# A second attention of its own: scores and maxima of two heads on the two row halves of TensorE, 1,024-column maxima, three score banks

## The chip, the cores and the metric

The kernel runs on one core of one Trainium2 chip. The metric is the device time of one execution in microseconds (us); lower is better. The core has TensorE for matmuls (PE in the rows, PEld for its weight loads), VectorE (DVE), ScalarE (ACT), GpSimd (POOL) and SyncE (SP). Each works through its own queue in order, and they wait for each other through semaphores. PSUM has eight banks of 512 f32 columns per partition.

## The reference, cut to what matters

A batch of 8 images of 32 x 32 positions with 192 channels passes through two attentions and a mixture of 16 experts. Both attentions have 12 heads of 16 channels and attend over the 1,024 positions of an image. The change is in the second one alone:

```
t = x.reshape(8, 1024, 192)
q, k, v = heads(ln(t) @ Wq + bq), heads(ln(t) @ Wk + bk), heads(ln(t) @ Wv + bv)
scores = einsum('bhqd,bhkd->bhqk', q, k) / sqrt(192)
t = t + (softmax(scores) @ v)
```

`L1_attn_ref` has `S = 1024` here, so each of the 96 (image, head) pairs has a 1024 x 1024 score matrix. The softmax needs the largest score of each query before it exponentiates.

## The kernel before

**Stages.** Projection and first attention (with position terms), projection and second attention, a router and the experts. `attention()` serves both attentions; `rel=False` is the second, and all that follows speaks of that one.

**Steps and blocks.** A step is one image and four heads (`GH = 4`), so there are `STEPS = 24` of them, two per trip of a loop (`ITERS = 12`; the first and the last trip are written out). A step has 16 blocks: a block is one tile of 128 keys (`kt`) against 512 queries (`qh`), for the four heads.

**Operands.** Queries and keys are kept as sums of two f16 parts, so a product has several terms, one for each pair of parts, stacked along the contraction: four terms of 16 rows here, 64 rows, and one more row (65) that subtracts the maximum, in the query operand `A`, against a constant row in `K`. A separate set of operands, `AM` and `KM`, feeds the maxima, with two heads on rows 0 to 63 and two on rows 64 to 127.

**Scores and exponentials.** In each block PE computes four heads' scores, 512 columns each, as two pairs (`scores_pair`, L371) into `psS`, four banks, two pairs deep: pair n waits until the exponential of pair n - 2 is done. ACT takes a pair in one instruction of 1,024 columns (L458) into `probs`. The product with the values (`pv`, L382) comes one block later: four heads in f32 on the four column groups of 32, eight matmul instructions in the trace, accumulating into the one bank `psO`.

**Maxima.** They are computed one step ahead, in the layout with queries on the partitions: 64 jobs per step, each one matmul of 512 keys (L353) into a ring of three banks, `psR`, and one DVE reduction of 512 columns (L503). Four jobs run in each block. When all 64 are done, DVE combines halves (L508), PE transposes the 32 columns once (`rows`, L357), DVE scales them (L513), and SP writes them by DMA into row 64 of `A` (L266). Each step also has two `back` jobs, one per query half: ACT copies `psO` out (L449), PE transposes it (four transposes, L361), DVE divides by the row sum (L520, L523), SP stores it.

**Order on PE in a block.** Both score pairs, two maxima jobs, `pv` of the block before, two more maxima jobs, then a `back` or `rows` job where there is one. The prologue, before step 0, has 77 jobs: all 64 of step 0, its `rows`, and 12 of step 1. The last step has no maxima left to compute.

**Loads.** POOL issues the DMAs for the next step one block at a time, each after a `pv`: eight of 128 KB for `A` and `K` (L185, L186), two for the values, and sixteen of 64 KB for `AM` and `KM` (L201, L202).

Of the kernel before, what the change touches and what calls it, by code (L numbers as in the profile page):

```python
# [6 lines left out]
F32 = mybir.dt.float32  # L7
F16 = mybir.dt.float16
I32 = mybir.dt.int32
ALU = mybir.AluOpType  # L10
ACT = mybir.ActivationFunctionType
AX = mybir.AxisListType

P = 128
# [4 lines left out]
GH = 4  # L19
# [23 lines left out]
def attention(nc, name, rel, scale, QK, RL, RLH, VN, OD, onehot_dram, head, early=None):  # L43
# [13 lines left out]
    with ExitStack() as ctx:  # L57
# [86 lines left out]
        def base_of(i):  # L144
            return BASE1 + (i - 1) * N_BODY
# [347 lines left out]
        @block.vector  # L493
        def _(dve):
            nc.vector.sem_inc(pvdone, 2)
            nc.vector.sem_inc(ring_free, 3)

            def job(jn, j, base, slot, buf, steps):
                dve.wait_ge(ring_full, base + jn + 1)
                if j[0] == "max":  # L500
                    r, half, p, qt, unit = max_of(j[1])
                    mx = MX[(buf + j[2]) % 2]
                    nc.vector.tensor_reduce(mx[:, unit, half:half + 1], psR[:, slot, :], AX.X, ALU.max)\  # L503
                        .then_inc(ring_free, 1)
                    if j[1] == HALVES - 1:

                        dve.wait_ge(ring_free, base + jn + 4)
                        nc.vector.tensor_tensor(MC[:, :], mx[:, :, 0], mx[:, :, 1], ALU.max).then_inc(maxed, 1)  # L508
                elif j[0] == "rows":

                    if steps is not None:
                        dve.wait_ge(mrow, steps * (16 * NROW) + 16 * NROW)
                    nc.vector.tensor_scalar(MT[:, :], psR[0:UNITS, slot, 0:P], -1.0 / MAXSCALE, None, ALU.mult)\  # L513
                        .then_inc(ring_free, 1)
                else:

                    qh, half = j[2], steps * QH + j[1] * QH + j[2]
                    o = psR[:, slot, :].rearrange("p (x v) -> p x v", v=VW)
                    dve.wait_ge(ring_free, base + jn + 3)
                    nc.vector.reciprocal(RC[:, :, :], o[:, :, HD:HD + 1]).then_inc(recips, 1)  # L520
                    dve.wait_ge(recips, half + 1)
                    dve.wait_ge(stored[qh], steps * 16 + (16 * j[1] + 16))
                    nc.vector.tensor_tensor(OS[:, qh, :, :], o[:, :, 0:HD], RC[:, :, :].to_broadcast([P, 4 * GH, HD]),  # L523
                                            ALU.mult).then_inc(ring_free, 1)

            for n, j in enumerate(FIRST):
                job(n, j, 0, first_slot(n), 0, None)

            def step(i, u, jobs, base, slot):
                for js in jobs[u]:  # L530
                    for jn, j in js:
                        job(jn, j, base, slot(jn), u, 2 * i + u)

            for u in range(2):
                step(0, u, JOBS_FIRST, BASE0, lambda n: first_slot(BASE0 + n))
            with dve.Fori(1, ITERS - 1) as i:
                for u in range(2):
                    step(i, u, JOBS, base_of(i), slot_of)
            for u in range(2):
                step(ITERS - 1, u, JOBS_LAST, base_of(ITERS - 1), slot_of)  # L540

def project(nc, name, first, IN, W, CONST, QK, VN, head, RL=None, RLH=None, ON=None, X2=None):
# [1088 lines left out]
class Head:  # L1632

    def __init__(self, nc, ctx, name, rel, QK, RL, RLH, onehot):
        def sb(n, shape, dt):
            return ctx.enter_context(nc.sbuf_tensor(f"{name}_{n}", shape, dt))

        def sem(n):
            return ctx.enter_context(nc.semaphore(f"{name}_{n}"))  # L1640

        self.rel, self.QK, self.RL, self.RLH, self.onehot = rel, QK, RL, RLH, onehot
        self.AM = [sb(f"qmax0_{h}", [P, 2, L], F16) for h in range(2)] if rel else [sb("qmax0", [P, 2, L], F16)] * 2
        self.KM = sb("kmax0", [P, 2, L], F16)
        self.MX = sb("halfmax0", [P, GH * KT, 2], F32)
        self.MC = sb("rowmax", [P, GH * KT], F32)
        self.MT = sb("rowmaxT", [GH * KT, P], F16)
        self.ident = sb("ident", [P, P], F32)
        self.loadedm = sem("loadedm0")
        self.const_km = sem("const_km0")  # L1650
        self.qkst, self.vst, self.xst = sem("qkst"), sem("vst"), sem("xst")
        self.last = sem("last")
        self.XST = ROUNDS * 384 - 192 + 16 if rel else ROUNDS * 64 + 16
        self.LAST = 96 + (192 if rel else 0)

    def wait_projected(self, engine):
# [2 lines left out]
        engine.wait_ge(self.xst, self.XST)  # L1659
        engine.wait_ge(self.last, self.LAST)  # L1660

    def load(self, pool):

        def pair(part, kind, r):
            return self.QK[0, part, kind].rearrange("(r p d) t -> r d p t", p=2, r=2)[r]
# [2 lines left out]
            k, t = rows.shape  # L1669
            return rows.rearrange("k (o t) -> k o t", o=1).to_broadcast([k, n, t])  # L1670

        KM, onehot = self.KM, self.onehot
        pool.wait_ge(self.qkst, 192 + 16)
        pool.wait_ge(self.vst, 96 + 16)
        if not self.rel:
            for n, (a, k) in enumerate(((0, 0), (0, 1), (1, 0), (1, 1))):
                for r in range(2):
                    of = slice(64 * r + HD * n, 64 * r + HD * n + HD)
                    pool.dma_start(self.AM[0][of, :, :], pair(a, 0, r)).then_inc(self.loadedm, 16)
                    pool.dma_start(KM[of, :, :], pair(k, 1, r)).then_inc(self.loadedm, 16)  # L1680
            return
        for r in range(2):
            at = 64 * r + HD
            pool.dma_start(KM[at:at + WI, :, :], every(onehot[HI:REL, :], 2)).then_inc(self.const_km, 16)
            for half in range(2):
                cols = slice(512 * half, 512 * half + 512)
                pool.dma_start(KM[at + WI:64 * r + 64, :, cols], every(onehot[16 * half:16 * half + 16, cols], 2))\
                    .then_inc(self.const_km, 16)
# [45 lines left out]
def hybrid_block(nc, a, out):  # L1734
# [21 lines left out]
    with ExitStack() as ctx:  # L1756
        head = Head(nc, ctx, "h2", False, QK2, None, None, a["onehot"])
        project(nc, "p2", False, a["x"], {"wqk": a["a_wqk"], "bqk": a["a_bqk"], "wv": a["a_wv"], "bv": a["a_bv"],
                                          "proj_w": a["proj_w"], "proj_b": a["proj_b"]}, const, QK2, VN2, head,
                ON=O1, X2=X2)  # L1760
        early = Early(nc, ctx, X2, ((a["w1"], a["b1"]), (a["w2"], a["b2"])))
        TR = ctx.enter_context(nc.sbuf_tensor("f_tileExpert", [1, P], I32))
        IXA = ctx.enter_context(nc.sbuf_tensor("f_slotsAll", [P, NTILE], I32))
        attention(nc, "a2", False, 1.0 / float(np.sqrt(C)), QK2, None, None, VN2, O2, a["onehot"], head, early)
        route(nc, "r", early, O2, a["wg"], a["bg"], X3, SLOTS, TR, IXA)
        experts(nc, "e", X3, early.W, early.wl, early.WDONE, TR, IXA, out)

# [51 lines left out]
```

## Time and profile before

| | |
|---|---|
| time, median of 3 runs | 3236.21 us (3226.59 to 3236.48) |
| the profiled execution: span, first to last instruction | 3278.2 us |
| mean granted TensorE clock | 0.906 of full speed |
| second attention: first maxima matmul to last transpose | 1750.0 to 2844.8 us |
| PE, DVE, ACT busy in 2000 to 2100 us | 99.6, 97.0, 73.0 us |

A row of the timeline gives the start, the length, the engine and line, output from input, and the number of like instructions that it merges; in square brackets, how long the engine had sat idle and what released it.
### The profile page before, as it was taken

How to read it: one execution, taken by the hardware profiler on the slowest of the kernel's cores; microseconds unless marked ns; L12 is line 12 of the kernel's file. 1: busy time of each engine (PE TensorE's matmuls, PEld its weight loads, DVE VectorE, ACT ScalarE, POOL GpSimd, SP SyncE). 2: the span in 40 equal slices, each digit the busy share in tenths (PEclk: the TensorE clock that was granted, in tenths of full speed). 3: DMA queues.
4: the chain of work that ended last, by engine and by line, in shares of the span. 5: the costliest groups of instructions: out<-in, count | busy, mean ns of one | idle time of the engine just before them, and what ended most of it. 6: DMA issues, size and time to landing. Idle time of an engine off the chain costs nothing. (4 is left out here: it accounts for less than half of the span.)

```text
span 3278.2 us, 63755 instructions
## 1 busy us (share of the span) xinstructions
PE 2922.2 (89%) x17818; PEld 1147.0 (35%) x17818; DVE 2439.8 (74%) x4430; ACT 1849.7 (56%) x2379; POOL 1061.6 (32%) x1714
## 2 busy tenths in 40 slices
PE   5886999999999999977897999999999999871887
PEld 4664122222222222215652222222222222361666
DVE  4544899999999999933547999999999999451221
ACT  2433376667776677663440677777777777610332
POOL 0012233333333333213232333232333332155665
PEclk9776799999999999998995999999999999965777
DMA  6776554555445554433654622222222222350211
GB/s 126 219 237 184 104 103 98 100 110 107 102 101 100 111 103 100 90 61 121 206 160 98 124 72 70 72 75 75 73 76 75 70 71 63 97 89 12 58 54 35
DMA packets 222364, 327.92 MB, mean 100 GB/s; under 512 B 63820, under 2 KB 150550, under 8 KB 217650
## 3 DMA queue, kind: packets, MB, share of 16 engines
q0 software_dynamic: 79488, 202.00, 27.3%
q1 hardware_dynamic: 142772, 124.60, 14.5%
q8 instruction: 56, 0.92, 0.1%
q14 instruction: 48, 0.39, 0.1%
HBM read 217.71 MB, written 109.19 MB: 100 GB/s over the span
## 5 line engine op out<-in xcount | busy, mean ns | idle before, releaser
L458 ACT ACTIVATE a_probs<-a_psS 128x1024 f32<-128x1024 f32 x1536 | 1488.5, 1021 | 738.5 <-PE a_psS L371 734.0
L503 DVE TENSOR_REDUCE h_halfmax<-a_psR 128x1 f32<-128x512 f32 x1536 | 979.7, 686 | 73.5 <-PE a_psR L353 64.3
L503 DVE TENSOR_REDUCE a_halfmax<-a_psR 128x1 f32<-128x512 f32 x1536 | 984.2, 686 | 63.6 <-PE a_psR L353 54.5
L371 PE MATMUL a_psS<-a_qrows,a_krows 121*128 121x512 f16 (+1 forms) x3072 | 804.2, 383 | 44.8 <-DMA a_qrows<-relh 40.2
L382 PE MATMUL a_psO<-a_probs,a_v 128*32 128x512 f32 x6144 | 824.0, 609 | 1.2 <-ACT a_probs L458 1.2
L353 PE MATMUL a_psR<-h_kmax,h_qmax 64*128 64x512 f16 x1536 | 357.9, 405 | 40.8 <-POOL h_ident L39 40.1
L371 PEld LDWEIGHTS a_psS<-a_qrows,a_krows 121*128 121x128 f16 (+1 forms) x3072 | 241.8, 98 | 417.7 <-issue 161.5
L353 PE MATMUL a_psR<-a_kmax,a_qmax 64*128 64x512 f16 x1536 | 325.6, 393 | 1.8 <-DVE a_halfmax L503 1.4
L353 PEld LDWEIGHTS a_psR<-h_kmax,h_qmax 64*128 64x128 f16 x1536 | 81.9, 93 | 539.1 <-DVE h_halfmax L503 471.6
L353 PEld LDWEIGHTS a_psR<-a_kmax,a_qmax 64*128 64x128 f16 x1536 | 78.9, 93 | 490.4 <-DVE a_halfmax L503 460.1
L185 POOL DMA_DIRECT2D a_qrows<-qk x240 | 124.1, 517 | 264.5 <-PE a_psO L382 262.0
L861 PE MATMUL p_psQ<-p_xnT,p_wqk 96*128 96x512 f32 x384 | 183.0, 640 | 16.0 <-DVE p_xnT L1015 13.9
L382 PEld LDWEIGHTS a_psO<-a_probs,a_v 128*32 128x32 f32 x6144 | 121.2, 108 | 183.3 <-issue 176.3
L201 POOL DMA_DIRECT2D h_qmax<-qk x110 | 56.3, 512 | 358.4 <-PE a_psO L382 305.2
L1628 DVE TENSOR_TENSOR e_y<-e_psY,e_x 128x192 f32<-128x192 f32 x80 | 28.6, 357 | 191.1 <-PE e_psY L1553 106.6
L201 POOL DMA_DIRECT2D a_qmax<-qk x120 | 61.4, 512 | 301.3 <-PE a_psO L382 300.5
L1049 DVE SCALAR_TENSOR_TENSOR p_half<-p_qk,p_sc,p_half 128x2048 f16<-128x2048 f32 (+1 forms) x36 | 71.5, 1997 | 103.1 <-ACT p_half L958 103.1
L951 ACT ACTIVATE p_qk<-p_psQ,p_bqk 128x512 f32<-128x512 f32 x96 | 65.9, 686 | 114.6 <-PE p_psQ L861 114.6
L1590 ACT COPY e_xmT<-e_psX 96x256 f32<-96x256 f32 x80 | 29.5, 369 | 175.0 <-PE e_psX L1547 130.5
L861 PEld LDWEIGHTS p_psQ<-p_xnT,p_wqk 96*128 96x128 f32 x384 | 77.5, 206 | 117.1 <-issue 107.3
L190 POOL DMA_DIRECT2D a_qrows<-rel x96 | 48.6, 506 | 205.6 <-PE a_psO L382 205.6
L197 POOL DMA_DIRECT2D a_v<-v x96 | 53.8, 560 | 185.4 <-PE a_psO L382 184.7
(185 smaller groups left out, 2755.2 us busy)
## 6 DMA issues: line engine op xcount, KB each, us to landing
a_qrows<-qk POOLq DMA_DIRECT2D x240, 128.0 KB, 4.2
qk<-p_half SPq DMA_DIRECT2D x96, 256.0 KB, 3.3
a_qrows<-rel POOLq DMA_DIRECT2D x96, 256.0 KB, 4.2
a_v<-v POOLq DMA_DIRECT2D x96, 256.0 KB, 3.1
a_krows<-qk POOLq DMA_DIRECT2D x168, 128.0 KB, 4.5
v<-p_v SPq DMA_DIRECT2D x36, 512.0 KB, 5.7
relh<-p_rel SPq DMA_DIRECT2D x48, 256.0 KB
attn<-a_out SPq DMA_DIRECT2D x96, 128.0 KB, 2.3
```

Of the source, the lines that this page charges most:

```text
L185: pool.dma_start(A[buf][c][at, :, :], qk(s, TERMS[n][0], 0)).then_inc(loaded[buf], 16)
L190: pool.dma_start(A[buf][c][w:w + WI, :, :], rel_w(s, half)).then_inc(loaded[buf], 16)
L197: pool.dma_start(V[buf][:, x, :, :], VN[s][:, x, :, :]).then_inc(loaded[buf], 16)
L201: pool.dma_start(AM[buf][0][of, :, :], qk_pair(s, TERMS[n][0], 0, r)).then_inc(loadedm[buf], 16)
L353: mm = nc.tensor.matmul(psR[:, slot, :], AM[b][half][at, p, P * qt:P * qt + P], KM[b][at, p, 512 * half:512 * half + 512], start=True, sto ...
L371: mm = nc.tensor.matmul(psS[:, (2 * n + j) % 4, :], K[buf][:, h, keys], A[buf][kt % NA][:, h, queries], start=True, stop=True)
L382: mm = nc.tensor.matmul(psO[32 * h:32 * h + 32, :], V[buf][:, kt, h, :], PT[:, blk % 2, h, :], start=(kt == 0), stop=(kt == KT - 1))
L458: nc.scalar.activation(PT[:, blk % 2, 2 * pair:2 * pair + 2, :], psS[:, b0:b0 + 2, :], ACT.Exp, scale=scale).then_inc(exped, 1)
L503: nc.vector.tensor_reduce(mx[:, unit, half:half + 1], psR[:, slot, :], AX.X, ALU.max)\
L861: mm = nc.tensor.matmul(psQ[:, n % 2, :], WQK[:, c, P * m:P * m + P], XN[:, c, 512 * q:512 * q + 512], start=(c == 0), stop=(c == 1))
L951: nc.scalar.activation(QF[:, m, 512 * q:512 * q + 512], psQ[:, n % 2, :], ACT.Identity, bias=BQK[:, m:m + 1], scale=1.0).then_inc(qf, 1)
L1049: half = nc.vector.scalar_tensor_tensor(HL[1][:, m, tokens], QF[:, m, tokens], SC[:, m:m + 1], HL[0][:, m, tokens], ALU.mult, ALU.subtract)
```

## The change

The second attention gets a function of its own, `attention_pairs`; the first keeps `attention()`.

- Three terms instead of four: 48 rows, 49 with the maximum's row. Heads 0, 1 lie on rows 0 to 48 and heads 2, 3 on rows 64 to 112, so that two heads' matmuls can run side by side. The same operands `A` and `K` serve scores and maxima; `AM` and `KM` are gone.
- Maxima: a job is two matmuls, one per row half, into 1,024 columns (two banks) of a ring of two, and one DVE reduction of 2 x 512 columns. There are 32 jobs per step, two per block, and the prologue has 22.
- Scores: two heads at a time, into a ring of three banks, and ACT takes one head of 512 columns per instruction. A pair of score matmuls waits until the first head of the pair before it has been exponentiated. The order in a block is: pair, maxima job, pair, maxima job (and `back`), `pv`.
- The maxima's row is made in two halves per step, after blocks 5 and 13: four small transposes into a score bank, an ACT copy, two DMAs.
- The twelve loads of `A` and `K` for the next step, 64 KB each, are issued together at the step's start; PE waits for them at block 5. The values are loaded after blocks 6 and 8.

```diff
+def attention_pairs(nc, name, scale, QK, VN, OD, onehot_dram, head, early):
+    TERMS = ((0, 0), (0, 1), (1, 0))
+    R = len(TERMS) * HD
+    HALF = PAIRS * 2 * KT // QH
+    PER_BLK = QH * HALF // BLK
+    NEXT = 5
+    AHEAD = NEXT + HALF // PER_BLK
+    EARLY = PER_BLK * (BLK - AHEAD)
+    RING = 2
+    BANKS = 3
...
+        psR = ctx.enter_context(nc.psum_tensor(f"{name}_psR", [P, RING, 1024], F32))
+        psS = ctx.enter_context(nc.psum_tensor(f"{name}_psS", [P, BANKS, 512], F32))
...
+        PROLOGUE = HALF + EARLY
...
+        def bank(m):
+            return (m + 1) % BANKS
...
+            def step(s, u, first):
+                for blk in range(BLK):
+                    if blk == 0 and not first:
+                        pool.wait_ge(scores, s * SCORES + 1)
+                        nc.gpsimd.sem_inc(paced, 1)
+                        head.load_step(pool, s + 1, A[1 - u], K[1 - u], loaded[1 - u])
...
+            def job(n, j, base, slot, buf, halves):
+                pe.wait_ge(ring_free, base + n + 1)
+                if j[0] == "max":
+                    qh, t, pair, kh, _ = max_of(j[1])
+                    b, q = (buf + j[2]) % 2, 512 * qh + P * t
+                    for r in range(2):
+                        of = slice(64 * r, 64 * r + R)
+                        mm = nc.tensor.matmul(psR[:, slot, 512 * r:512 * r + 512], A[b][of, pair, q:q + P],
+                                              K[b][of, pair, 512 * kh:512 * kh + 512], start=True, stop=True)
...
+            def two_scores(s, buf, kt, qh, pair, m, first):
+
+                if not (first and m == 0):
+                    pe.wait_ge(exped, s * SCORES + m)
+                keys, queries = slice(P * kt, P * kt + P), slice(512 * qh, 512 * qh + 512)
+                for r in range(2):
+                    of = slice(64 * r, 64 * r + R + 1)
+                    nc.tensor.matmul(psS[:, bank(m + r), :], K[buf][of, pair, keys], A[buf][of, pair, queries],
+                                     start=True, stop=True).then_inc(scores, 1)
...
+                for blk in range(BLK):
+                    kt, qh = blk % KT, blk // KT
+                    if blk == NEXT and not end:
+                        pe.wait_ge(loaded[1 - u], i * NLOAD + (1 + u) * NLOAD)
+                    if blk == KT:
+                        pe.wait_ge(mrow, s * (QH * NROW) + QH * NROW)
+                    for pair in range(PAIRS):
+                        two_scores(s, u, kt, qh, pair, place(blk, 2 * pair, end), start)
+                        for n, j in jobs[u][blk][:1] if pair == 0 else jobs[u][blk][1:]:
+                            job(n, j, base, (n + shift) % RING, u, s * QH)
...
+                    if blk >= 1:
+                        pv(s, u, i, blk - 1, end)
...
+                for blk in range(BLK):
+                    for o in range(GH):
+                        m = place(blk, o, end)
+                        act.wait_ge(scores, s * SCORES + m + 2)
+                        if o == 0:
+                            act.wait_ge(pvdone, s * PVS + blk + 1)
+                        nc.scalar.activation(PT[:, blk % 2, o, :], psS[:, bank(m), :], ACT.Exp, scale=scale)\
+                            .then_inc(exped, 1)
...
-        attention(nc, "a2", False, 1.0 / float(np.sqrt(C)), QK2, None, None, VN2, O2, a["onehot"], head, early)
+        attention_pairs(nc, "a2", 1.0 / float(np.sqrt(C)), QK2, VN2, O2, a["onehot"], head, early)
```

`exped` counts finished exponentials and starts at 1 through the row of the prologue, so the wait for `s * SCORES + m` before scores m and m + 1 means that score m - 2 has been exponentiated.

## Rows read from the trace of the kernel before

**Rows 1.** Windows: busy us (instructions) of PE, PEld, DVE, ACT, POOL; clock; DMA.
```profile
2000.00:2100.00 100.00, 99.57 (x608) 26.88 (x604) 96.98 (x162) 72.95 (x79) 31.12 (x61) 1.00 0.29 76
```

**Rows 2.** Timeline of one block of the loop, and the next block's first row.
```profile
2001.90 1.06 PE L382 MATMUL a_psO<-a_probs,a_v 128*32 128x512 f32 x8
2002.90 0.39 PE L353 MATMUL a_psR<-a_kmax,a_qmax 64*128 64x512 f16 x2
2003.22 1.04 PE L371 MATMUL a_psS<-a_qrows,a_krows 65*128 65x512 f16 x4
2003.68 0.51 POOL L185 DMA_DIRECT2D a_qrows<-qk  x1 [1.40 <-PE a_psO L382]
2003.95 1.94 ACT L458 ACTIVATE a_probs<-a_psS 128x1024 f32<-128x1024 f32 x2 [0.75 <-PE a_psS L371]
2004.19 0.39 PE L353 MATMUL a_psR<-a_kmax,a_qmax 64*128 64x512 f16 x2
2004.29 0.51 POOL L186 DMA_DIRECT2D a_krows<-qk  x1
2004.52 1.06 PE L382 MATMUL a_psO<-a_probs,a_v 128*32 128x512 f32 x8
```

**Rows 3.** PE timeline of a block that has a back job.
```profile
2028.03 0.66 PE L361 MATMUL a_psR<-h_ident,a_outT 128*128 128x128 f32 x4
2028.53 1.03 PE L371 MATMUL a_psS<-a_qrows,a_krows 65*128 65x512 f16 x4
```

**Rows 4.** The once-a-step transpose of the maxima: five steps, first and last start.
```profile
L357 PE MATMUL a_psR<-h_ident,h_rowmax x5: 284/284/284, 2014.0 to 2189.2; 128*32 128x128 f32 x5
```

**Rows 5.** Groups by form, 1800 to 2900 us: busy, mean ns of one.
```profile
L458 ACT ACTIVATE a_probs<-a_psS 128x1024 f32<-128x1024 f32 x766 | 742.3, 1021 | 275.4 <-PE a_psS L371 273.2
L503 DVE TENSOR_REDUCE a_halfmax<-a_psR 128x1 f32<-128x512 f32 x755 | 483.9, 686 | 18.7 <-PE a_psR L353 14.2
L449 ACT COPY a_outT<-a_psO 128x512 f32<-128x512 f32 x48 | 28.4, 591 | 2.9 <-PE a_psO L382 1.8
L1392 DVE TENSOR_REDUCE r_top<-r_isTop 128x16 f32<-128x256 f32 x1 | 0.4, 420 | 0.0
```

**Rows 6.** Timeline of the last step, where no maxima are left.
```profile
2803.67 3.91 ACT L458 ACTIVATE a_probs<-a_psS 128x1024 f32<-128x1024 f32 x4 [1.02 <-PE a_psS L371]
2807.62 0.11 PEld L371 LDWEIGHTS a_psS<-a_qrows,a_krows 65*128 65x128 f16 x2 [0.32 <-ACT a_probs L458]
...
2814.13 1.04 PE L371 MATMUL a_psS<-a_qrows,a_krows 65*128 65x512 f16 x4
2814.77 3.90 ACT L458 ACTIVATE a_probs<-a_psS 128x1024 f32<-128x1024 f32 x4 [0.79 <-PE a_psS L371]
```

**Rows 7.** Timeline of the prologue: first maxima, a run of them, first scores, a lone matmul.
```profile
1750.01 1.03 PE L353 MATMUL a_psR<-h_kmax,h_qmax 64*128 64x512 f16 x3 [20.18 <-POOL h_ident L39]
1790.33 7.27 DVE L503 TENSOR_REDUCE a_halfmax<-a_psR 128x1 f32<-128x512 f32 x12 [0.26 <-PE a_psR L353]
...
1796.40 1.89 PE L371 MATMUL a_psS<-a_qrows,a_krows 65*128 65x512 f16 x4
...
1799.61 0.61 PE L353 MATMUL a_psR<-a_kmax,a_qmax 64*128 64x512 f16 x1 [0.36 <-DVE a_halfmax L503]
```

**Rows 8.** Timeline of the end: the maxima's last transpose, the last back job.
```profile
2801.83 0.27 PE L357 MATMUL a_psR<-h_ident,h_rowmax 128*32 128x128 f32 x1 [0.73 <-DVE h_rowmax L508]
...
2844.20 0.63 PE L361 MATMUL a_psR<-h_ident,a_outT 128*128 128x128 f32 x4 [0.80 <-ACT a_outT L449]
```

**Rows 9.** Windows at half clock and in the last step, columns as in Rows 1.
```profile
1801.00:1806.00 5.00, 5.00 (x18) 0.97 (x17) 2.62 (x5) 1.95 (x3) 0.69 (x2) 0.50 0.01 3
...
2810.00:2835.00 25.00, 24.44 (x148) 5.62 (x148) 1.36 (x4) 22.78 (x26) 0.00 (x0) 1.00 0.03 11
```

**Rows 10.** DMA issues: KB each, median us to landing.
```profile
h_qmax<-qk POOLq DMA_DIRECT2D x144, 64.0 KB, 2.3
```

More of the change, by code:

```diff
@@ L1642, in __init__ @@
         self.rel, self.QK, self.RL, self.RLH, self.onehot = rel, QK, RL, RLH, onehot
[L1643 to L1650, printed above, removed]
+        if rel:
+            self.AM = [sb(f"qmax0_{h}", [P, 2, L], F16) for h in range(2)]
+            self.KM = sb("kmax0", [P, 2, L], F16)
+            self.MX = sb("halfmax0", [P, GH * KT, 2], F32)
+            self.MC = sb("rowmax", [P, GH * KT], F32)
+            self.MT = sb("rowmaxT", [GH * KT, P], F16)
+            self.ident = sb("ident", [P, P], F32)
+            self.loadedm = sem("loadedm0")
+            self.const_km = sem("const_km0")
+        else:
+            self.A = sb("qrows0", [P, 2, L], F16)
+            self.K = sb("krows0", [P, 2, L], F16)
+            self.loaded = sem("loaded0")
         self.qkst, self.vst, self.xst = sem("qkst"), sem("vst"), sem("xst")
@@ L1660, in wait_projected, with load_step @@
         engine.wait_ge(self.last, self.LAST)
+    def load_step(self, pool, s, A, K, done):
+        for n, (a, k) in enumerate(((0, 0), (0, 1), (1, 0))):
+            for r in range(2):
+                of = slice(64 * r + HD * n, 64 * r + HD * n + HD)
+                pool.dma_start(A[of, :, :], self.QK[s, a, 0].rearrange("(r p d) t -> r d p t", p=2, r=2)[r]).then_inc(done, 16)
+                pool.dma_start(K[of, :, :], self.QK[s, k, 1].rearrange("(r p d) t -> r d p t", p=2, r=2)[r]).then_inc(done, 16)
     def load(self, pool):
@@ L1670, in every @@
             return rows.rearrange("k (o t) -> k o t", o=1).to_broadcast([k, n, t])
-        KM, onehot = self.KM, self.onehot
         pool.wait_ge(self.qkst, 192 + 16)
@@ L1675, in load @@
         if not self.rel:
[L1676 to L1680, printed above, removed]
+            self.load_step(pool, 0, self.A, self.K, self.loaded)
             return
+        KM, onehot = self.KM, self.onehot
         for r in range(2):
```

305 lines of the change are left out of this document (added).

## The prediction
> **What bounds the kernel now.** I read the windows first, then the timeline of single blocks, then the groups for the lengths of single instructions. The windows show PE busy all the time, DVE nearly so, and ACT at three quarters [rows 1]. PE and DVE cannot both be the limit, and the busy shares do not decide it, because instructions overlap at their ends. The timeline does. PE's groups in a block follow each other without a pause: from `pv` to the next maxima 1.00 us, maxima to scores 0.32, scores to maxima 0.97, maxima to `pv` 0.32 to 0.33, together 2.62 us [rows 2]. DVE's four reductions would allow less: in the prologue they follow each other every (7.27 - 0.69) / 11 = 0.60 us [rows 5, 7], 2.39 us a block. ACT needs 2 x 0.92 = 1.84 us: two exponentials end 1.94 us after the first starts and one lasts 1.02 [rows 2, 5]. So the second attention is bound by PE's order of work, a step takes (2189.2 - 2014.0) / 4 = 43.8 us [rows 4], and PE has no slack to give away.
>
> Two sizes of PE are needed. Four score matmuls take 1.04 us and one takes 0.39, so they follow each other every 0.22 us [rows 2]. Two maxima matmuls on different row halves take together 0.39 us, as long as one [rows 2]: they do run side by side. And a change of group costs about 0.10 us over the streaming (0.32 - 0.22 for the maxima). In the prologue the third maxima matmul, on the row half of the first, ends 1.03 us after the first starts, and one alone lasts 0.61 there: 0.42 apart, which is 512 columns at 1.2 GHz, so between groups with the same row halves there is no such cost [rows 7].
>
> **PE's work shrinks.** Per block it becomes: pair 0.22, maxima 0.22, pair 0.22, maxima 0.32 (then the shape changes), `pv` 1.00: 1.98 us against 2.62. Dropping the fourth term changes no column count, so by itself it gives nothing.
>
> **DVE's work shrinks a little.** The trace has no reduction of 1,024 columns. From 256 to 512 columns it grows by 686 - 420 = 266 ns [rows 5], so 512 more make the step between two reductions 0.60 + 0.53 = 1.13 us, 2.26 a block. The Trainium skill ("Perfetto Trace Analysis", Optimizing Scalar/DVE Operations) says that grouping into larger operations pays if the engine is saturated, and gives about 125 ns of fixed cost for DVE on PSUM. By that figure 32 fewer instructions would save 4.0 us a step. By the rows they save 32 x (2 x 0.60 - 1.13) = 2.2 us. The trace agrees with the direction and not with the size, and neither counts here, because DVE is not what ends last.
>
> **ACT's work grows, and its latency comes onto PE's path.** An exponential of 512 columns is not in the trace; the copy of 512 columns from PSUM takes 0.59 us and the exponential of 1,024 takes 1.02 [rows 5]. The lower bound is half of 1.02 (0.51), the upper 0.69, DVE's time for the same columns; I take 0.59, the same engine and size. ACT's rate is not the problem: it has 0.59 - 0.10 = 0.49 us per head, 1.96 a block. The ring is. A block's second pair may start only when the first head of its first pair has been exponentiated, and that pair was issued just before. The loop is: score matmul 0.39, ACT's start after it, exponential 0.59, PE's start after that. In the written-out steps ACT starts 0.64 us after a pair that takes 0.22 + 0.39 = 0.61, so some 0.04 late [rows 6]. In the loop it starts 2003.95 - 2003.22 = 0.73 us after, some 0.13 late, since it works out two semaphore values there [rows 2]; the first head of a block has the same two waits after the change. PE's weight load starts 0.04 to 0.05 us after the exponential's end (2803.67 + 3.91 = 2807.58, then 2807.62) [rows 6]. Together 0.39 + 0.13 + 0.59 + 0.05 = 1.16 us in the loop, 1.07 written out.
>
> During this PE has only one maxima job of 0.22 us to do. What is queued behind the waiting pair is the second maxima job, `pv` and the next block, so all of them are late. From the second pair to the next block's first pair PE needs 0.22 + 0.32 + 1.00 = 1.54 us. **A block therefore takes 1.16 + 1.54 = 2.70 us in the loop and 2.61 written out**, against 2.62 now. The other ring does not bind: a job's slot is free 0.22 + 0.39 + 0.04 + 1.22 = 1.87 us after the block's start (a reduction of 1,024 lasting 0.69 + 0.53), and its next user comes at 2.9. Bounds: with 0.51 for the exponential a block takes 2.62, with 0.69 it takes 2.80, with 0.10 more for a change of group between pair and maxima 2.80.
>
> **Extras of a step.** A `back` job costs 0.50 us of transposes (2028.03 to 2028.53) and now waits for its slot in the shorter ring some 0.3, 0.8 each [rows 3]. Each half row of maxima puts four transposes of 128 columns on PE, 0.11 us each like those of `back`, and a change of group: 0.55; there are two. ACT's copy of `psO` now meets the next pair: 0.15, twice. Step in the loop: 16 x 2.70 + 1.6 + 1.1 + 0.3 = 46.2 us, written out 16 x 2.61 + 3.0 = 44.8. Before 43.8 [rows 4].
>
> **The sum.** ACT's loop covers steps 4 to 21: 18 x 2.4 = +43 us. Steps 0 to 3 and most of 22: 5 x 1.0 = +5. From the last maxima transpose to the last back job it takes 2844.2 - 2801.8 = 42.4 us now [rows 8], with blocks of about 2.1 since no maxima are left. After: one `pv` 1.0, two blocks of step 22 5.2, five blocks with maxima 13.1, eleven without (1.07 + 0.32 + 1.00 = 2.39) 26.3, extras 2.0, the end 2.0: 49.6, so +7. The prologue now takes 1796.40 - 1750.01 = 46.4 us [rows 7]. After: 22 jobs at 1.13 us, of which the scores need to wait for 20: 0.64 + 19 x 1.13 + 1.22 + 0.5 = 23.8, so -22.5. The waiting for the row of maxima (job 17, then a transpose, a copy, and a DMA of some 2.3 us as the 64 KB ones [rows 10]) ends at about the same time. Step 0 runs at half clock at first, now as then [rows 9]; I count no difference. Sum 43 + 5 + 7 - 22.5 = +32 us. On the profiled execution: 3278.2 + 32 = 3310 us of span. That execution lies 42 us above the median of the runs; the difference is counted in us, so the median becomes 3236.2 + 32 = **3268 us**.
>
> **Rivals.** *The wait is shorter (no change).* If the first exponential starts 0.04 late in the loop too, 18 x 16 x 0.09 = 26 us go, and the time is 3242. Against it: the code has the same two waits. Speaking for it: the exponential's price is a copy's. Chance 0.17.
>
> *The rings do not bind (faster).* Then DVE's two reductions end last, 2.26 us a block, 38 us a step with the back jobs: 23 x -5.8 - 22.5 = -156, 3080 us. It decides if PE can write a pair while the pair before it is still unread. The wait on the count rules that out, but part of it would do: below about 1.07 us for the wait of 1.16 the sum turns negative. With every term at its low bound (exponential 0.51, start 0.04, no idle back jobs) it is 0.17 x 288 + 0.08 x 90 + 9 = 65 less, 3203. Chance 0.10 for anything faster.
>
> *The clock falls.* PE now idles 0.5 us in every block. In the last step of before it also waits for ACT, and the granted clock stays 1.00 with 148 matmuls in 25 us; after the change a block has 16 in 2.70, the same 148 in 25 [rows 9]. That speaks against it. The Trainium skill ("TensorE: Matmul & The Clock Gate", A second HAM failure mode: psum-queue depth-cycling) says that frequent short idling between groups of matmuls, while PSUM banks are cycled, can make the clock swing between its two levels. Were it so for half of the time, a block at half clock would take 0.61 + 0.13 + 0.59 + 0.05 + 0.43 + 0.54 + 1.86 = 4.2 us, 1.5 more than 2.70, and 192 blocks cost 290 us: 3560. The half-clock lengths are twice the streamed columns plus the same change of group. Chance 0.05.
>
> *The loads come late.* Twelve DMAs issued 0.6 us apart [rows 2] and landing 2.3 us later [rows 10] are there 9.5 us after a step's start; PE asks at 5 x 2.70 + 0.8 = 14.3. Only landings three times as long would show, at about 2 us a step: 3310. Chance 0.05.
>
> **Chances and range.** Forecast 0.63; the rest as above. A measurement of this kernel tells 0.3% (10 us) from no change. The forecast's own spread, 3247 to 3295, spills little into "same": faster 0.10, same 0.20, slower 0.70. The range 3225 to 3312 takes in the shorter wait and late loads, and leaves out a fallen clock and most of the faster cases.
>
> **What would show it.** Right: `pv` to `pv` 2.70 us in the loop and 2.61 in the first steps; PE idle about 0.5 us before each block's second pair, released by ACT's exponential; DVE idle about 0.4 us a block; exponentials of 0.59 us; first scores about 24 us after the first maxima; granted clock 1.00. Wrong: exponentials longer or shorter than 0.59, a pair of score matmuls longer than 0.39, a clock below 1.00 after step 0, a PE wait for a load at block 5.

## The result, and the profile after

| | before | after |
|---|---|---|
| median of the timed runs | 3231.20 us (5 runs, 3226.59 to 3236.48) | 3297.91 us (5 runs, 3291.69 to 3314.40) |
| the profiled execution: time, span | span 3278.2 us | 3314.4, 3311.9 us |
| mean granted clock | 0.906 | 0.915 |

The ratio after / before is 1.021, with a 95% interval of 1.018 to 1.023: the change costs 67 us. Forecast were 3268 us (3225 to 3312), slower with 0.7.

The windows of the kernel after, columns as in [rows 1]: one of a quiet stretch, one of 1,000 us of the attention, and three around the moment when ACT's loop jumps back.

```profile
1900.00:2000.00 100.00, 81.16 (x604) 18.80 (x597) 87.22 (x83) 80.53 (x151) 15.09 (x29) 1.00 0.13 41
1850.00:2850.00 1000.00, 793.34 (x5740) 182.94 (x5738) 843.09 (x803) 769.47 (x1435) 152.33 (x294) 0.98 0.14 43
2060.00:2069.00 9.00, 5.94 (x46) 1.23 (x43) 6.66 (x6) 5.92 (x12) 2.70 (x6) 1.00 0.32 92
2069.00:2077.00 8.00, 7.32 (x36) 1.00 (x32) 4.26 (x4) 4.95 (x10) 3.43 (x7) 0.57 0.23 72
2077.00:2085.00 8.00, 6.53 (x52) 1.61 (x48) 7.21 (x8) 5.54 (x11) 0.00 (x0) 1.00 0.05 17
```

PE was busy 99.6 of 100 us before [rows 1] and is so 81.2 now. No engine took its place at 100: DVE stands at 87 and ACT at 81. Such a page, with three engines at four fifths, is what a loop of waits looks like: each engine waits for another in turn.

The timeline of one block after, which answers to [rows 2] (weight loads left out):

```profile
2007.52 1.06 PE L795 MATMUL a_psO<-a_probs,a_v 128*32 128x512 f32 x8
...
2008.52 0.39 PE L773 MATMUL a_psS<-h_qrows,h_krows 49*128 49x512 f16 x2
...
2008.74 0.38 PE L757 MATMUL a_psR<-a_krows,a_qrows 48*128 48x512 f16 x2
2009.02 2.16 ACT L872 ACTIVATE a_probs<-a_psS 128x512 f32<-128x512 f32 x4 [0.53 <-PE a_psS L773]
2009.17 2.38 DVE L923 TENSOR_REDUCE a_halfmax<-a_psR 128x2 f32<-128x1024 f32 x2 [0.31 <-PE a_psR L757]
...
2009.67 0.39 PE L773 MATMUL a_psS<-h_qrows,h_krows 49*128 49x512 f16 x2 [0.55 <-ACT a_probs L872]
...
2009.90 0.38 PE L757 MATMUL a_psR<-a_krows,a_qrows 48*128 48x512 f16 x2
...
2010.21 1.06 PE L795 MATMUL a_psO<-a_probs,a_v 128*32 128x512 f32 x8
```

From `pv` to `pv` 2010.21 - 2007.52 = 2.69 us. Of that 1.15 lie between the first pair (2008.52) and the second (2009.67), and in them PE idles 0.55, released by ACT's exponential; the remaining 1.54 pass without a pause. DVE idles 0.31 and ACT 0.53 in the same block.

The groups of the page that price the two new instructions, and PE's timeline at the first maxima, the first scores and the last transposes (as [rows 7] and [rows 8]):

```profile
L923 DVE TENSOR_REDUCE a_halfmax<-a_psR 128x2 f32<-128x1024 f32 x768 | 915.6, 1225 | 177.6 <-PE a_psR L757 168.0
L872 ACT ACTIVATE a_probs<-a_psS 128x512 f32<-128x512 f32 x1536 | 830.2, 595 | 241.5 <-PE a_psS L773 226.5
```

```profile
1768.64 1.03 PE L757 MATMUL a_psR<-h_krows,h_qrows 48*128 48x512 f16 x4 [21.59 <-POOL a_ident L39]
...
1792.68 0.64 PE L773 MATMUL a_psS<-h_qrows,h_krows 49*128 49x512 f16 x2
...
2922.80 0.63 PE L762 MATMUL a_psR<-a_ident,a_outT 128*128 128x128 f32 x4 [0.80 <-ACT a_outT L854]
```

These give the two profiled executions stage by stage:

| stretch | before | after | difference |
|---|---|---|---|
| up to the first maxima (code not changed) | 1750.0 | 1768.6 | +18.6 |
| first maxima to first scores | 46.4 | 24.0 | -22.4 |
| first scores to the last back job | 1047.8 | 1130.1 | +82.3 |
| from there to the end (code not changed) | 434.0 | 389.1 | -44.9 |

The last line is not the change's. The router and the experts take 383 to 392 us in the profiled executions of the kernel after and of the eleven kernels below, and 434 in before's own, which stood 42 us above before's median; the timed executions of before do not have these 45 us. In that one the granted clock is 0.5 for 269 of the 434 us, in after's for 160 of the 389. The spans differ by 33.7 us, which looks like the forecast of +32 and is a coincidence; the attention itself is 60 us longer, and the medians differ by 67. The 7 us between these two are not assigned to a stage.

### The profile page after: what moved, and what is told of

It is laid out like the page before. It is cut to its first block and busy times, and to the rows that moved or that the text cites. A ratio compares the mean times of both kernels' runs of the same rounds, so it can differ in the third digit from the quotient of the medians.

```text
span 3311.9 us, 62012 instructions
## 1 busy us (share of the span) xinstructions
PE 2731.7 (82%) x17986; PEld 1035.9 (31%) x17986; DVE 2384.9 (72%) x3662; ACT 1955.0 (59%) x3195; POOL 913.2 (28%) x1426
## 5 line engine op out<-in xcount | busy, mean ns | idle before, releaser
L923 DVE TENSOR_REDUCE a_halfmax<-a_psR 128x2 f32<-128x1024 f32 x768 | 915.6, 1225 | 177.6 <-PE a_psR L757 168.0
L458 ACT ACTIVATE a_probs<-a_psS 128x1024 f32<-128x1024 f32 x768 | 744.2, 1021 | 401.1 <-PE a_psS L371 398.9
L872 ACT ACTIVATE a_probs<-a_psS 128x512 f32<-128x512 f32 x1536 | 830.2, 595 | 241.5 <-PE a_psS L773 226.5
L503 DVE TENSOR_REDUCE h_halfmax<-a_psR 128x1 f32<-128x512 f32 x768 | 490.1, 685 | 58.8 <-PE a_psR L353 54.3
L503 DVE TENSOR_REDUCE a_halfmax<-a_psR 128x1 f32<-128x512 f32 x768 | 492.6, 686 | 45.5 <-PE a_psR L353 40.9
L371 PE MATMUL a_psS<-a_qrows,a_krows 121*128 121x512 f16 x1536 | 404.7, 385 | 45.7 <-DMA a_qrows<-relh 43.5
L773 PE MATMUL a_psS<-h_qrows,h_krows 49*128 49x512 f16 x768 | 155.2, 401 | 112.8 <-ACT a_probs L872 112.6
L353 PE MATMUL a_psR<-h_kmax,h_qmax 64*128 64x512 f16 x768 | 181.0, 409 | 20.4 <-POOL h_ident L39 20.0
L757 PE MATMUL a_psR<-h_krows,h_qrows 48*128 48x512 f16 x768 | 157.2, 406 | 31.9 <-POOL a_ident L39 21.6
L353 PE MATMUL a_psR<-a_kmax,a_qmax 64*128 64x512 f16 x768 | 163.5, 395 | 0.9 <-DVE a_halfmax L503 0.7
```

What stands on the lines that cost most here:

```text
L353: mm = nc.tensor.matmul(psR[:, slot, :], AM[b][half][at, p, P * qt:P * qt + P], KM[b][at, p, 512 * half:512 * half + 512], start=True, sto ...
L371: mm = nc.tensor.matmul(psS[:, (2 * n + j) % 4, :], K[buf][:, h, keys], A[buf][kt % NA][:, h, queries], start=True, stop=True)
L458: nc.scalar.activation(PT[:, blk % 2, 2 * pair:2 * pair + 2, :], psS[:, b0:b0 + 2, :], ACT.Exp, scale=scale).then_inc(exped, 1)
L757: mm = nc.tensor.matmul(psR[:, slot, 512 * r:512 * r + 512], A[b][of, pair, q:q + P], K[b][of, pair, 512 * kh:512 * kh + 512], start=True, ...
L773: nc.tensor.matmul(psS[:, bank(m + r), :], K[buf][of, pair, keys], A[buf][of, pair, queries], start=True, stop=True).then_inc(scores, 1)
L872: nc.scalar.activation(PT[:, blk % 2, o, :], psS[:, bank(m), :], ACT.Exp, scale=scale)\
```

## The experiments

The questions were: is it the wait for the first head that lengthens the block, and what is the rest, 28 us, that the forecast's blocks do not hold? Each kernel is the kernel after with the edit shown, except that e9's edit is shown against e8. The reference time is that of the kernel before, run beside them, with medians of 3228 to 3231 us.

**The rest: where the trace shows it.** After's blocks are 2.69 us almost everywhere, but some are 4.0 to 4.6. PE and ACT timelines around one of them:

```profile
2066.24 0.39 PE L773 MATMUL a_psS<-h_qrows,h_krows 49*128 49x512 f16 x2
...
2068.16 2.16 ACT L872 ACTIVATE a_probs<-a_psS 128x512 f32<-128x512 f32 x4 [1.95 <-issue]
...
2068.81 0.39 PE L773 MATMUL a_psS<-h_qrows,h_krows 49*128 49x512 f16 x2 [1.97 <-ACT a_probs L872]
...
2069.35 1.86 PE L795 MATMUL a_psO<-a_probs,a_v 128*32 128x512 f32 x8
```

The scores are there from 2066.2 on, and ACT starts on them at 2068.16 only, after an idle of 1.95 us that no semaphore explains ("issue"). It happens eight times between 2065 and 2742 us, 94 to 99 us apart, which is one trip of two steps, so at the jump back of ACT's loop (here at 2065.3 us); and the waits of 1830 to 2890 us have it as one line (in total, times, longest):

```profile
PE a_psS L773 <- ACT a_probs L872: 209.8, 359, 2.0
```

```profile
ACT a_probs L872 <- issue: 15.1, 8, 2.0
```

The DMA queue that brings ACT's instructions in, in the stretch 1965 to 2765 us, first of before and then of after (packets, MB, share):

```profile
q14 instruction: 1, 0.01, 0.0%
```

```profile
q14 instruction: 41, 0.34, 0.1%
```

```profile
2166.38 1.93 PE L795 MATMUL a_psO<-a_probs,a_v 128*32 128x512 f32 x8
...
2169.62 0.60 PE L773 MATMUL a_psS<-h_qrows,h_krows 49*128 49x512 f16 x2 [0.34 <-ACT a_probs L872]
...
2170.58 1.93 PE L795 MATMUL a_psO<-a_probs,a_v 128*32 128x512 f32 x8
```

Eight pauses of about 1.4 us make 11, and 47.8 us at 4.20 instead of 2.69 a block lose 47.8 x (1 - 2.69 / 4.20) = 17: together 28 us, the whole rest.

**e1: ACT's loop written out.**

```diff
-            with act.Fori(2, ITERS - 1) as i:
+            for i in range(2, ITERS - 1):
```

> ACT's loop over steps 4 to 21 is written out, so that ACT works with constants and never jumps back; nothing else changes. Theory A (the ring of three banks sets the block: first score matmul, first exponential, second pair) says that ACT's start in these steps falls from 0.13 to 0.04 us after the matmul, the block from 2.69 to 2.61 us, 18 steps x 16 x 0.08 = 23 us less. Theory B (each jump back of ACT's loop waits for its code, about 2 us late, and the idle PE then loses its clock for a while) says that the gaps of over 4 us between two pv disappear, the granted clock stays 1.00 from step 1 to the end of the attention, and about 29 us more go. Both: 3298 - 52 = 3246 us. If the late starts and the clock have another cause (loads, the maxima's row), only the 23 us go: 3275 us.

Measured: 3251.96 us (3245.31 to 3264.41), 1.007 of before (1.005 to 1.009), so 46 us under after. Windows and a block of it:

```profile
1850.00:2850.00 1000.00, 812.75 (x6028) 189.71 (x6032) 871.31 (x836) 810.06 (x1512) 153.47 (x296) 1.00 0.15 44
```

```profile
2206.93 0.39 PE L773 MATMUL a_psS<-a_qrows,a_krows 49*128 49x512 f16 x2
...
2208.00 0.39 PE L773 MATMUL a_psS<-a_qrows,a_krows 49*128 49x512 f16 x2 [0.47 <-ACT a_probs L872]
```

Pair to pair 1.07 us and a block 2.61, as forecast for written-out code. No late start, a clock of 1.00 for 1,000 us, every step of the loop's stretch 45.05 us, although PE idles 0.47 us in each block. Two things went at once here, the pauses and the two values that ACT works out; e5 parts them.

**e5: one wait per pair instead of one per head**, which shortens the loop and keeps it.

```diff
-                        act.wait_ge(scores, s * SCORES + m + 2)
+                        if o % 2 == 0:
+                            act.wait_ge(scores, s * SCORES + m + 3)
```

> ACT keeps its loop, but waits once for both scores of a pair instead of once for each, so that its loop has about 80 instructions fewer of 314. Theory A: the first exponential starts 3 ns later at most, block unchanged at 2.69. Theory B: if the shorter loop fits where the code is kept, the code is not fetched again in each trip, the eight late starts and the falls of the clock go, 29 us less: 3269 us; if it still doesn't fit, no change. Without theory B: no change, 3298 us.

Measured: 3278.33 us (3268.18 to 3286.62), 1.015 (1.013 to 1.017), 20 us under after. ACT now waits for both heads of a pair, and the block is 0.03 us longer, 2.72; steps take 46.56 us, all of them. No instruction packet comes in for ACT between 2030 and 2765 us, there is no late start, and the clock is 1.00:

```profile
1850.00:2850.00 1000.00, 790.23 (x5866) 184.82 (x5864) 868.41 (x819) 789.46 (x1466) 152.71 (x296) 1.00 0.14 43
```

A trip of ACT's loop has 250 instructions in e5, against 314. So the pause does not come with looping as such, and the fallen clock belongs to the pause and not to the idling in each block. That it is the length of the loop rests on the packets and on this one edit, which also takes out half of ACT's waits; a loop of 314 instructions with e5's waits was not run.

**e2 and e3: shorten the exponential of one head** to 256 of its 512 columns, the first head of a block (e2) or the fourth (e3, `o == 3`). Both leave work out: the other 256 columns keep what `probs` held before.

```diff
+                        n = 256 if o == 0 and not (first and u == 0) else 512
-                        nc.scalar.activation(PT[:, blk % 2, o, :], psS[:, bank(m), :], ACT.Exp, scale=scale)\
+                        nc.scalar.activation(PT[:, blk % 2, o, 0:n], psS[:, bank(m), 0:n], ACT.Exp, scale=scale)\
```

> From step 1 on, the first head's exponential of each block covers 256 of its 512 columns (the rest of that head's probabilities are left out). Theory A: 256 columns are 0.21 us of the loop that PE waits for, so the block falls from 2.69 to 2.48 us, 368 x 0.21 = 77 us less: 3221 us. Rival (ACT's amount of work sets the block): the same 77 us. Rival (DVE or PE's own work sets it): no change, 3298 us.

> As before, but the fourth head's exponential of each block is the one that covers 256 of 512 columns: the same work left out, at a place where no pair of scores waits for it. Theory A: no change within 10 us, 3298 us. Rival (ACT's amount of work sets the block): 77 us less, as with the first head's.

Measured: e2 3216.29 us (3209.36 to 3231.11), 0.997 (0.995 to 0.998); e3 3292.11 us (3286.82 to 3312.79), 1.019 (1.017 to 1.021). The second pair of e2 and of e3, with the start of their first pairs at 2206.61 and 2206.92:

```profile
2206.61 0.39 PE L773 MATMUL a_psS<-a_qrows,a_krows 49*128 49x512 f16 x2
...
2207.55 0.39 PE L773 MATMUL a_psS<-a_qrows,a_krows 49*128 49x512 f16 x2 [0.33 <-ACT a_probs L873]
```

```profile
2206.92 0.39 PE L773 MATMUL a_psS<-h_qrows,h_krows 49*128 49x512 f16 x2
...
2208.07 0.39 PE L773 MATMUL a_psS<-h_qrows,h_krows 49*128 49x512 f16 x2 [0.55 <-ACT a_probs L873]
```

The same work taken from ACT is worth 0.21 us a block in the first head and nothing in the fourth. What counts is ACT's latency for one head and not its rate. The Trainium skill ("Perfetto Trace Analysis", Optimizing Scalar/DVE Operations) says that breaking up instructions of ScalarE or VectorE can help where they aren't saturated and cause bubbles on another engine; e2 agrees in direction (0.94 us from pair to pair instead of 1.15), but it leaves work out, and a first head in two whole pieces was not tried.

**e4 and e6: give the waiting time work.** Both maxima jobs go between the pairs, in e6 with ACT's loop written out as well.

```diff
-                        for n, j in jobs[u][blk][:1] if pair == 0 else jobs[u][blk][1:]:
+                        for n, j in jobs[u][blk][:PER_BLK] if pair == 0 else jobs[u][blk][PER_BLK:]:
```

> Only PE's order within a block changes: both maxima jobs of a block are issued after its first pair of scores, where PE waits for the first exponential, instead of one after each pair. Theory A: the wait of 1.15 us from the first pair to the second stays and now hides both jobs; from the second pair to the next block's first PE needs 0.32 + 1.00 instead of 0.22 + 0.32 + 1.00, so the block falls from 2.69 to 2.47 us, 368 x 0.22 = 81 us less: 3217 us, with the late starts of ACT's loop as before. Rival (PE's own amount of work or DVE sets the block, the wait fills what is left): no change, 3298 us. Rival (the two slots of the maxima's ring now bind): the second job waits up to 0.15 us, which the wait of 1.15 hides; if it didn't, 3250 us.

> The order of the run before this one, and ACT's loop written out. Theories A and B add up: block 1.07 + 0.32 + 1.00 = 2.39 us, no gaps of over 4 us, clock 1.00: 3252 - 81 = 3171 us, faster than both kernels. If the two don't add (DVE's 2.26 us a block and its divisions come close), 3190 us.

Measured: e4 3224.72 us (3212.51 to 3236.11, 10 runs), 0.998 (0.997 to 1.000); e6 3182.50 us (3176.51 to 3195.86), 0.985 (0.983 to 0.986). A block of e6:

```profile
2207.14 1.06 PE L795 MATMUL a_psO<-a_probs,a_v 128*32 128x512 f32 x8
...
2208.36 0.83 PE L757 MATMUL a_psR<-h_krows,h_qrows 48*128 48x512 f16 x4
...
2209.21 0.39 PE L773 MATMUL a_psS<-h_qrows,h_krows 49*128 49x512 f16 x2
...
2209.53 1.06 PE L795 MATMUL a_psO<-a_probs,a_v 128*32 128x512 f32 x7
```

The four maxima matmuls lie under the wait, the wait itself does not change, and the block shrinks from 2.61 to 2.39 us. In e4 it is 2.47, but ACT's late starts are all there (eight, up to 2.45 us), five of them with gaps of over 4 us between two `pv`, and the clock falls twice. Both came 8 to 11 us above what was expected. Their plain blocks are as expected, but two kinds of block do not shrink with them. One with a `back` job takes 3.52 us in e1 and in e6 alike: its transposes wait for a slot of the maxima's ring (PE idles 0.25 us before them in e1, 0.42 in e6). One with a row's transposes goes from 3.14 to 3.09. Each stands twice in a step, so a step falls from 45.05 to 42.33 us, 2.7 us instead of 16 x 0.22 = 3.5, which over 23 steps is more than the 8 to 11 us.

**e7 and e8: a fourth score bank.** The maxima go one head at a time into a ring of three banks; a pair may then start when the pair two before it is exponentiated. e8 has ACT's loop written out.

```diff
-    RING = 2
-    BANKS = 3
+    RING = 3
+    BANKS = 4
...
-                    pe.wait_ge(exped, s * SCORES + m)
+                    pe.wait_ge(exped, s * SCORES + m - 1)
```

> One part of the change undone: the maxima go back to reductions of 512 columns in a ring of three banks, 64 jobs a step, four a block, and the bank that this frees makes the ring of scores four banks, so that a pair waits for the pair two before it. Rows halves, 49 rows, 512-column exponentials and the rest stay. Theory A: PE no longer waits for the exponential of the pair just issued; DVE's 4 x 0.60 = 2.39 us becomes the bound of a block, against 2.69, so 0.29 x 368 = 107 us less, 2 us more prologue: 3193 us with the late starts of ACT's loop, which may now be partly hidden. Rival (the wait is not the cause): the block stays at 2.7 us or rises with DVE's longer work: 3298 us or more.

> Four score banks and 512-column maxima as in the run before this one, and ACT's loop written out. Theory A: the start of the exponential is no longer on the path, so writing the loop out brings nothing but theory B's 29 us: 3164 us. If the deeper ring hides the late starts, no more than the run before: 3193 us.

Measured: e7 3272.05 us (3269.56 to 3279.07), 1.013 (1.011 to 1.014); e8 3270.31 us (3263.24 to 3284.18), 1.014 (1.011 to 1.016). They came 79 and 106 us above what was expected of them. PE's rows of a block of e7:

```profile
2208.90 0.39 PE L772 MATMUL a_psS<-a_qrows,a_krows 49*128 49x512 f16 x2
...
2209.13 0.38 PE L756 MATMUL a_psR<-a_krows,a_qrows 48*128 48x512 f16 x2
...
2209.35 0.38 PE L772 MATMUL a_psS<-a_qrows,a_krows 49*128 49x512 f16 x2
...
2209.57 0.38 PE L756 MATMUL a_psR<-a_krows,a_qrows 48*128 48x512 f16 x1
...
2210.29 0.39 PE L756 MATMUL a_psR<-a_krows,a_qrows 48*128 48x512 f16 x1 [0.35 <-DVE a_halfmax L922]
...
2210.61 1.07 PE L794 MATMUL a_psO<-a_probs,a_v 128*32 128x512 f32 x8
```

The wait for ACT is gone: the second pair starts 0.45 us after the first. But all four maxima are queued within 0.7 us, the fourth needs the slot of the first, and `pv` is queued behind it. The block takes 2.70 us again, now by the other ring. The expectation had counted DVE's rate and not its latency, the same mistake one ring further. ACT's late starts (seven, up to 2.7 us) cost 0.5 to 1.0 us each here, since two pairs lie ready and PE idles less than 1 us behind them; the clock stays at 1.00, and writing the loop out brings nothing that the medians show.

**e9: four banks with the order of before** (both pairs, two maxima, `pv`, two maxima), ACT's loop written out. The edit is against e8.

```diff
                     for pair in range(PAIRS):
                         two_scores(s, u, kt, qh, pair, place(blk, 2 * pair, end), start)
-                        for n, j in jobs[u][blk][:2] if pair == 0 else jobs[u][blk][2:]:
-                            job(n, j, base, (n + shift) % RING, u, s * QH)
+                    for n, j in jobs[u][blk][:2]:
+                        job(n, j, base, (n + shift) % RING, u, s * QH)
...
+                    for n, j in jobs[u][blk][2:]:      # after pv
+                        job(n, j, base, (n + shift) % RING, u, s * QH)
```

> Four score banks and 512-column maxima with ACT's loop written out, as in the run that came out at 3270, but PE's order within a block is that of the kernel before: both pairs, two maxima jobs, pv, two maxima jobs. Theory A, as the last traces leave it: PE's order puts the wait of some ring on PE's path, and there it was the maxima's ring of three, whose fourth job came 0.7 us too early. With pv between the second and third job that wait lies behind pv: PE needs 1.98 us a block, DVE 2.39, and DVE sets the block at 2.39 to 2.45: 3270 - 0.28 x 368 = 3167 us, up to 3185. Rival (work on 512 columns, not the order, costs what the last two runs showed): 3270 us.

Measured: 3206.23 us (3192.35 to 3217.15), 0.992 (0.990 to 0.994): 64 us better than e8 by order alone, and 20 to 40 above what was expected. DVE's row of a block says why:

```profile
2204.80 4.46 DVE L924 TENSOR_REDUCE a_halfmax<-a_psR 128x1 f32<-128x512 f32 x7
```

Seven reductions with no idle time between them, (4.46 - 0.69) / 6 = 0.63 us each on average, four to a block of 2.48: with reductions of one head DVE is busy to the end of every block. Not all of it is DVE's own rate. Three of four reductions start 0.60 us after the one before, as in [rows 7], but one in each block starts 0.68 after (2204.80, then 2205.48): its matmul stands behind `pv` on PE, starts at 2205.06 and is done just then. At 0.60 a block would be 2.39. Two of 1,024 columns take (4.61 - 1.22) / 3 = 1.13 us each in e10, 2.26 a block:

```profile
2205.77 4.61 DVE L934 TENSOR_REDUCE a_halfmax<-a_psR 128x2 f32<-128x1024 f32 x4
```

So by rate the merged reduction is worth 2.39 - 2.26 = 0.13 us a block, and against e9's block as it runs 0.22, once PE no longer waits.

**e10 and e11: split `pv` and fill both gaps.** With after's three banks, `pv` is done in two halves of 256 queries, one behind each pair and maxima job (whole in the first block of a half step, where the accumulation starts). ACT's loop is written out in both, in e11 PE's too.

```diff
-                for h in range(GH):
-                    mm = nc.tensor.matmul(psO[32 * h:32 * h + 32, :], V[buf][:, kt, h, :],
...
+                for part in (parts if kt else (None,)):
+                    q = slice(256 * part, 256 * part + 256) if kt else slice(0, 512)
+                    for h in range(GH):
+                        mm = nc.tensor.matmul(psO[32 * h:32 * h + 32, q], V[buf][:, kt, h, :],
...
+                        if pair == 0 and blk >= 1:
+                            pv(s, u, i, blk - 1, end, (0,))
...
-            with pe.Fori(1, ITERS - 1) as i:          # e11 only
+            for i in range(1, ITERS - 1):
```

> The changed kernel with ACT's loop written out and pv cut into two halves of 256 queries (except in the first block of each accumulation), one after each pair of scores, so that both waits for an exponential are covered by like amounts of work: 0.22 + 0.32 + 0.57 = 1.11 us each. Theory A: a block takes 2 x 1.11 = 2.22 us on PE, 2.26 on DVE, against 2.61, in 14 of 16 blocks, and the copy and divisions of a step as before: 3252 - 0.35 x 322 = 3139 us. Rival (twice as many f32 matmuls and weight loads cost more than their columns): up to 0.2 us more a block, 3205 us.

> As the run with pv in two halves, and PE's loop over steps 2 to 21 written out as well. In the trace of that run four of PE's jumps back to its loop's start (at 2266, 2431, 2518 and 2604 us) took some 5 us, with code packets landing just then, and the clock fell after each. Theory B, now for PE: without the jump these four go, some 6 us each, 3156 - 24 = 3132 us, and the clock stays 1.00 from step 1 to the end of the attention. Rival (a row of maxima or a load is late there, and the code packets only stand beside it): no change, 3156 us. Rival (PE's code written out doesn't come in fast enough): slower, with pauses all along.

Measured: e10 3155.56 us (3144.70 to 3173.19), 0.978 (0.975 to 0.981); e11 3132.17 us (3126.68 to 3141.82), 0.971 (0.969 to 0.972), the fastest of all and what was expected of it; e10 came 17 us above its 3139. PE in e11, then one place in e10:

```profile
2206.01 0.64 PE L801 MATMUL a_psO<-a_probs,a_v 128*32 128x256 f32 x8
2206.58 0.39 PE L773 MATMUL a_psS<-h_qrows,h_krows 49*128 49x512 f16 x2
2206.81 0.38 PE L757 MATMUL a_psR<-a_krows,a_qrows 48*128 48x512 f16 x2
2207.12 0.64 PE L801 MATMUL a_psO<-a_probs,a_v 128*32 128x256 f32 x8
```

```profile
2266.40 0.64 PE L801 MATMUL a_psO<-a_probs,a_v 128*32 128x256 f32 x8
...
2271.34 0.39 PE L773 MATMUL a_psS<-h_qrows,h_krows 49*128 49x512 f16 x2 [4.30 <-issue]
```

Half a block takes 1.11 us in both, without a pause on PE: half of `pv` stands where PE waited, so that the wait is covered from both sides. Splitting costs PE little: 0.57 us for each half against 1.00 for the whole. But it puts more instructions into PE's loop, and e10 pays for that as after does on ACT: at four of PE's own nine jumps back the next half block comes 4.4 to 4.8 us later than usual, with packets for PE's code in the loop, and the clock at half after each. In e11 the pauses are gone and the median is 23 us lower.

## Why the prediction was right in direction, and what it missed

- **The block** was forecast at 2.70 us in the loop and 2.61 written out; it is 2.69 and 2.61. Its parts hold as well: exponential 0.59 (595 ns), pair to pair 1.16 (1.15), the rest 1.54 (1.54). The reduction of 1,024 columns, worked out from a single one of 256 in the router, is 1.22 (1.225) and comes every 1.13 us (1.13 in e10). e2 and e3 show that the first head's latency is what counts, e4 and e6 that the time of the wait is empty.
- **The steps**, forecast at 46.2 and 44.8: one without a jump of ACT's loop in it takes 46.15 in the loop, and 45.05 written out (e1). Counted from `pv` to `pv`, the steps that hold one of the eight jumps take 47.7 to 52.5.
- **The prologue**, forecast at 23.8 us, takes 24.0. No load is waited for at block 5.
- **The sum** is where the prediction failed: +54.5 us from first scores to the end (its +32 without the prologue's gain) became +82.3. It took 18 steps at 46.2 and knew no step that is longer. The 28 us are ACT's eight late starts at the jump back and the clock at half behind them, as computed above: a term that the sum put at nothing. e1 takes 2869.8 - 1787.7 = 1082 us for this stretch; adding the 1.1 us that each of 18 loop steps takes more than a written-out one gives 1102, which is the forecast. The time of 3298 us lies above the forecast's own spread (3247 to 3295) and inside its range only because the range left room for late loads, and no load was late; that part is luck.
- **The rival "the clock falls"** had 0.05 and came true in part, by another way. It expected the idling of 0.5 us in each block to bring the clock down; e1 and e5 have that idling in every block and keep 1.00 for 1,000 us. Behind the eight pauses of about 2 us it did fall six times, and its length for a block at half clock, 4.2 us, is what the trace shows. The Trainium skill's account ("TensorE: Matmul & The Clock Gate", A second HAM failure mode: psum-queue depth-cycling), frequent short idling between groups while banks are cycled, is the case of e1 and e5, and there the traces show no swing.
- **The anchor.** The forecast added its difference to the median and took before's profiled execution as it stood. That execution had some 45 us in the experts that no other profiled one has. It did no harm to the forecast, but it hides the loss from whoever compares the two spans.
- **"The wait is shorter"** (3242 us) is not what happened: ACT starts 2009.02 - 2008.52 = 0.50 us after a pair's first matmul in after's loop and 0.42 in e1, and the two values are what makes it 2.69 instead of 2.61.

## What to carry to other kernels

When a ring becomes shorter or its users finer, compute the closed loop (producer, start, consumer, release) and ask how much work the producer has in the queue between two uses; e8 and e9 differ by 64 us in nothing but that order. Count the instructions of a hardware loop when a change makes them smaller and more numerous, and look at the instruction queues of the trace for packets inside the loop. Compare two profiled executions stage by stage before reading anything from their spans.

## What the runs showed of the hardware that was not expected

- Reductions of 512 columns follow each other every 0.60 us when the next one is ready in time, those of 1,024 every 1.13.
- The unchanged stages ahead of the attention took from 1750.0 to 1769.4 us in the profiled executions, and the router and the experts 434 us once and 383 to 392 otherwise, with the same code.
